# Five-stage transformer kernel on one Trainium2 core: two elementwise products and the low halves of the dispatch weights move from VectorE to GpSimd, and the input comes in three transfers

## The reference, cut to what matters

```python
x = x + 0.5 * L0_ffn(layernorm(x))     # fp4 feed-forward, "f0"
x = x + L0_attn(layernorm(x))          # decayed linear attention, "a0"
x = x + 0.5 * L0_ffn(layernorm(x))     # "f0" again
x = x + 0.5 * L1_ffn(layernorm(x))     # soft mixture of experts, "f1"
x = x + L1_attn(layernorm(x))          # causal softmax attention, 16 heads, "a1"
x = x + 0.5 * L1_ffn(layernorm(x))     # "f1" again

def fp4_quant_dequant(x):              # blocks of 16 along the last dimension
    scale = max(max(abs(xb)) / 6, 1e-12)
    idx = searchsorted(MID, abs(xb / scale))
    return GRID[idx] * sign(xb) * scale

def L0_ffn(x):                         # every operand is quantized first
    h = silu(q(x) @ q(w_gate).T) * (q(x) @ q(w_up).T)      # 704 wide
    return q(h) @ q(w_down).T

def L1_ffn(x):                         # 8 experts of 128 slots = 1024 slots
    logits = rms_norm(x, gamma_x) @ rms_norm(slot_embeds, gamma_slot).T
    dispatch = softmax of logits over the 8 experts
    slots = dispatch.T @ xn
    out = softmax over all 1024 slots of logits @ (gelu(slots @ w1) @ w2)
```

## Time and profile before

| What | Value |
|---|---|
| median of 3 executions | 2931.3 us |
| the profiled execution's own time | 2929.66 us |
| its span in the profile | 2927.6 us |
| PE / PEld busy | 2429.8 / 1846.8 us (83% / 63%) |
| DVE busy | 2108.1 us (72%) |
| ACT busy | 1625.4 us (56%) |
| POOL busy | 1096.1 us (37%) |
| mean granted clock of PE | 0.935 of 2.4 GHz |

### The profile page before, as it was taken

The page is one execution under the profiler, slowest core; times in us unless marked ns, Lnnn a source line. Parts: engine busy times, 40 slices in busy tenths (PEclk is TensorE's granted clock), DMA queues, the critical chain, the costliest instruction groups (busy, mean ns, idle before and its releaser), DMA issues.

```text
span 2927.6 us, 56018 instructions
## 1 busy us (share of the span) xinstructions
PE 2429.8 (83%) x23228; PEld 1846.8 (63%) x23228; DVE 2108.1 (72%) x3530; ACT 1625.4 (56%) x2761; POOL 1096.1 (37%) x791
## 2 busy tenths in 40 slices
PE   1677777778888988889889889889898888898888
PEld 0445555555666766657567666667666667677666
DVE  6599999889898886777877777776786765343432
ACT  2244544454765757365566556574656566556554
POOL 0144544444352443244443526262525252222112
PEclk9799998899999999989898999999989999999999
DMA  4000000000000000000000000000000000000000
GB/s 153 17 1 1 1 1 1 1 1 1 1 1 1 1 1 1 23 13 12 11 14 2 23 2 23 2 23 2 23 9 21 12 2 8 8 8 1 8 8 8
DMA packets 34572, 32.96 MB, mean 11 GB/s; under 512 B 7377, under 2 KB 33681, under 8 KB 34321
## 3 DMA queue, kind: packets, MB, share of 16 engines
q1 hardware_dynamic: 34320, 29.40, 3.1%
HBM read 12.34 MB, written 4.19 MB: 6 GB/s over the span
## 4 chain that ended last, share of the span: by engine, by line
PE 44%; DVE 17%; ACT 6%; issue 4%; POOL 4%; SPq 1%; DMA 1%; POOLq 0%; DVEq 0%; ACTq 0%
PE psum L623 11%; PE psum L625 10%; PE psum L624 10%; PE psum L629 3%; PE psum L1055 2%; DVE a1pr L1771 2%; PE psum L1057 2%; PE psum L1056 2%; POOL f1hT L2042 2%; PE psum L906 1%; PE psum L959 1%; DVE f1d L1882 1%; DVE a1c L1789 1%; PE psum L936 1%; DVE f1e L1886 1%
## 5 line engine op out<-in xcount | busy, mean ns | idle before, releaser
L2042 POOL TENSOR_TENSOR f1hT<-f1g,f1hT 128x512 f16<-128x512 f32 x256 | 311.7, 1224 | 677.1 <-ACT f1hT L1422 676.6
L2029 POOL TENSOR_TENSOR a1pr<-a1PT,a1pr 128x1024 f16<-128x1024 f32 (+1 forms) x176 | 350.3, 1992 | 334.9 <-DVE a1pr L1771 334.9
L623 PE MATMUL psum<-f1sl,f1w1h 128*128 128x256 f16 x1024 | 290.4, 284 | 30.7 <-DVE f1pr L1929 16.6
L623 PE MATMUL psum<-f1w2h,f1hT 128*128 128x256 f16 x1024 | 282.4, 276 | 17.0 <-POOL f1hT L2042 15.2
L624 PE MATMUL psum<-f1sl,f1w1h 128*128 128x256 f16 x1024 | 290.0, 283 | 0.0
L625 PE MATMUL psum<-f1sl,f1w1l 128*128 128x256 f16 x1024 | 289.7, 283 | 0.0
L624 PE MATMUL psum<-f1w2l,f1hT 128*128 128x256 f16 x1024 | 281.6, 275 | 0.0
L625 PE MATMUL psum<-f1w2h,f1hT 128*128 128x256 f16 x1024 | 281.4, 275 | 0.0
L1748 DVE TENSOR_REDUCE a1nm<-psum 128x2 f32<-128x768 f32 (+3 forms) x176 | 198.1, 1125 | 79.1 <-PE psum L886 77.7
L2006 POOL TENSOR_TENSOR f0hT<-f0Y,f0hT 128x512 f16<-128x512 f32 (+1 forms) x128 | 139.6, 1105 | 181.4 <-ACT f0Y L1214 181.4
L1771 DVE CAST a1pr<-a1PT 128x1024 f16<-128x1024 f32 (+1 forms) x176 | 156.0, 891 | 69.5 <-ACT a1PT L1318 49.5
(11 more groups left out here) (335 smaller groups left out, 7502.1 us busy)
## 6 DMA issues: line engine op xcount, KB each, us to landing
a1Q<-a1st SPq DMA_DIRECT2D x96, 64.0 KB, 2.6
a1K<-a1st SPq DMA_DIRECT2D x96, 64.0 KB, 2.5
x<-in_L_attn_x SPq DMA_DIRECT2D x8, 512.0 KB, 8.8
out<-x SPq DMA_DIRECT2D x8, 512.0 KB, 3.0
wslot<-in_L_ffn_w SPq DMA_DIRECT2D x1, 1024.0 KB, 7.5
wraw<-in_L_ffn_w SPq DMA_DIRECT2D x1, 1024.0 KB, 5.7
wslot<-in_L_ffn_slot_embeds SPq DMA_DIRECT2D x1, 1024.0 KB, 8.2
a1Q<-a1mr SPq DMA_DIRECT2D x64, 4.0 KB, 1.7
```

The source lines that it names most:

```text
L623: e.matmul(out, lh, rh, start=start, stop=False)
L2029: e.tensor_tensor(a1["pr"][:, i % 2, 1, :, 0:w], a1["PT"][:, i % 2, :, 0:w], a1["pr"][:, i % 2, 0, :, 0:w], ALU.subtract).then_inc(s["a1_pl"])
L2042: e.tensor_tensor(hT1[:, 1, 2 * hp:2 * hp + 2, :], gg[:, hp % 2, :, :], hT1[:, 0, 2 * hp:2 * hp + 2, :], ALU.subtract).then_inc(s["f1_hl"])
```

## The change

- `f0_tokens`, `f0_hidden`: the first product Y goes to POOL (`f0_products`, the new `f0_scaled`). What was one instruction with a scalar and a tensor factor becomes a small one of DVE, r = r * (-TIE), and a product of POOL. Two semaphores, `f0_xp` and `f0_hp`, tell DVE that Y is there; `f0_xm` and `f0_hm` now count two for each tile, one for r and one for M.
- `f1_weights`: the low half goes from DVE to POOL, with the same signal `f1_el`.
- `load`: sequence 0 alone, then sequences 1 to 3 in one transfer, then 4 to 7 in one; the last two are due behind the other weights. They are a chain of their own.

```diff
--- before.py
+++ after.py
@@ -396,10 +396,10 @@
         for name in (
                 "dve", "w_dma", "w_dma2", "w_dma3", "w_qm", "w_qr", "w_q", "w_sq", "w_pw", "w_se", "w_T", "w_h", "w_l", "w_b",
                 "w_sh", "w_sl", "w_k",
-                "xin0", "xin1", "xin2", "xin3", "out",
+                "xin0", "xin1", "xin2", "out",
                 "ln_ve", "ln_rs", "a0_ve", "a0_rs",
-                "f0_xm", "f0_xr", "f0_xy", "f0_xq", "f0_xT", "f0_xh", "f0_xl", "f0_g", "f0_u", "f0_si", "f0_th",
-                "f0_hm", "f0_hr", "f0_hy", "f0_hq", "f0_hT", "f0_hY", "f0_hl", "f0_dn", "f0_xu",
+                "f0_xp", "f0_xm", "f0_xr", "f0_xy", "f0_xq", "f0_xT", "f0_xh", "f0_xl", "f0_g", "f0_u", "f0_si", "f0_th",
+                "f0_hp", "f0_hm", "f0_hr", "f0_hy", "f0_hq", "f0_hT", "f0_hY", "f0_hl", "f0_dn", "f0_xu",
                 "a0_xn", "a0_xT", "a0_xh", "a0_xl", "a0_pj", "a0_sg", "a0_qr", "a0_qh", "a0_ql", "a0_kh", "a0_kl",
                 "a0_v", "a0_kt", "a0_a", "a0_vf", "a0_vb", "a0_vh", "a0_vl", "a0_nh", "a0_nl", "a0_af", "a0_ah",
                 "a0_al", "a0_y", "a0_yh", "a0_yl", "a0_kv", "a0_S", "a0_Sh", "a0_Sl", "a0_o", "a0_xu",
@@ -538,10 +538,9 @@
         def sync(e, q, banks):
 
             def load(b):
-                yield 0.5 if b < 2 else 6.0 + b
-                if b >= 4:
-                    q.wait_ge(f"xin{b % 4}", 16)
-                e.dma_start(xb[:, b, :, :], x_d[:, b, :, :]).then_inc(s[f"xin{b % 4}"], 16)
+                yield (0.5, 6.0, 9.0)[b]
+                bs = (slice(0, 1), slice(1, 4), slice(4, 8))[b]
+                e.dma_start(xb[:, bs, :, :], x_d[:, bs, :, :]).then_inc(s[f"xin{b}"], 16)
 
             def store(b):
                 yield at_f1(B + b) + 152.0
@@ -610,7 +609,7 @@
                 yield 1.0e6
                 q.wait_ge("out", 16 * B)
 
-            return [weights(), *[chain(z, B) for z in (load, a1_moves, store)], last()]
+            return [weights(), chain(load, 3), *[chain(z, B) for z in (a1_moves, store)], last()]
 
 
 
@@ -1173,7 +1172,7 @@
                     n = 2 * f + tp
                     yield S + 4.0 + 20.0 * tp
                     q.wait_ge("w_dma", 96)
-                    q.wait_ge("f0_xm", n + 1)
+                    q.wait_ge("f0_xm", 2 * n + 2)
                     e.activation(f0["Mx"][:, :], f0["Mx"][:, :], ACT.Relu, scale=MAGIC, bias=cst[:, C_MAG:C_MAG + 1]).then_inc(s["f0_xr"])
                     yield S + 7.8 + 20.0 * tp
                     q.wait_ge("f0_xT", n + 1)
@@ -1194,7 +1193,7 @@
                     e.activation(f0["h"][:, ft % 3, :].rearrange("p (i n) -> p i n", i=2), psum[:, 0:2, 0:FH], ACT.Silu,
                                  scale=1.0 / (XS * WS)).then_inc(s["f0_si"])
                     yield G + 8.0
-                    q.wait_ge("f0_hm", ft + 1)
+                    q.wait_ge("f0_hm", 2 * ft + 2)
                     m2 = f0["M"][:, t % 2, :]
                     e.activation(m2, m2, ACT.Relu, scale=MAGIC, bias=cst[:, C_MAG:C_MAG + 1]).then_inc(s["f0_hr"])
 
@@ -1541,7 +1540,7 @@
                 b = f % B
                 yield S
                 if f < B:
-                    q.wait_ge(f"xin{b % 4}", 16 * (b // 4 + 1))
+                    q.wait_ge(f"xin{(b > 0) + (b > 3)}", 16)
                 else:
                     q.wait_ge("a0_xu", 4 * b + 4)
                 normalize("x", b, "ln_ve")
@@ -1564,10 +1563,11 @@
                     q.wait_ge("dve", q.tick())
                     e.reciprocal(r_, c_).then_inc(s["dve"])
                     q.wait_ge("dve", q.tick())
-                    e.scalar_tensor_tensor(blocks16(Yx), blocks16(v), -TIE, bc(r_, 16), ALU.mult, ALU.mult).then_inc(s["dve"])
-                    q.wait_ge("dve", q.tick())
+                    e.tensor_scalar(r_, r_, -TIE, None, ALU.mult).then_inc(s["f0_xm"])
+                    yield S + 4.4 + 20.0 * tp
+                    q.wait_ge("f0_xp", n + 1)
                     e.tensor_scalar(Mx.bitcast(u32), Yx.bitcast(u32), 0x7F800000, None, ALU.bitwise_and).then_inc(s["f0_xm"])
-                    yield S + 4.6 + 20.0 * tp
+                    yield S + 5.6 + 20.0 * tp
                     q.wait_ge("f0_xr", n + 1)
                     e.scalar_tensor_tensor(Yx, Mx, MAGIC, Yx, ALU.add, ALU.add).then_inc(s["dve"])
                     q.wait_ge("dve", q.tick())
@@ -1602,10 +1602,9 @@
                     q.wait_ge("dve", q.tick())
                     e.reciprocal(r_, c_).then_inc(s["dve"])
                     q.wait_ge("dve", q.tick())
-                    e.scalar_tensor_tensor(blocks16(Y), blocks16(h), -TIE, bc(r_, 16), ALU.mult, ALU.mult).then_inc(s["dve"])
-                    k = q.tick()
-                    yield G + 7.2
-                    q.wait_ge("dve", k)
+                    e.tensor_scalar(r_, r_, -TIE, None, ALU.mult).then_inc(s["f0_hm"])
+                    yield G + 8.0
+                    q.wait_ge("f0_hp", ft + 1)
                     e.tensor_scalar(M.bitcast(u32), Y.bitcast(u32), 0x7F800000, None, ALU.bitwise_and).then_inc(s["f0_hm"])
                     yield G + 9.2
                     q.wait_ge("f0_hr", ft + 1)
@@ -1881,9 +1880,6 @@
                     q.wait_ge("f1_el", n)
                     e.tensor_tensor(d3, Lg[:, :, jp * 256:(jp + 1) * 256], psum[:, 4, 0:2 * P].unsqueeze(1).broadcast_to([P, NT, 2 * P]),
                                     ALU.subtract).then_inc(s["f1_ds"])
-                    yield E + 4.0
-                    q.wait_ge("f1_eh", n + 1)
-                    e.tensor_tensor(e1[:, jp % 2, 1, :, :], d3, e1[:, jp % 2, 0, :, :], ALU.subtract).then_inc(s["f1_el"])
 
             def f1_slots(j):
                 S = at_f1(j)
@@ -1980,9 +1976,21 @@
                 S = at_f0(f)
                 v = f0["xh"][:, :, :].rearrange("p t d -> p (t d)")
                 for tp in range(2):
+                    yield S + 3.2 + 20.0 * tp
+                    q.wait_ge("f0_xm", 2 * (2 * f + tp) + 1)
+                    e.tensor_tensor(blocks16(f0["Yx"][:, :]), blocks16(v), bc(f0["scx"][:, 1, :], 16), ALU.mult).then_inc(s["f0_xp"])
                     yield S + 5.6 + 20.0 * tp
                     q.wait_ge("f0_xy", 2 * f + tp + 1)
                     e.tensor_tensor(blocks16(v), blocks16(f0["Yx"][:, :]), bc(f0["scx"][:, 0, :], 16), ALU.mult).then_inc(s["f0_xq"])
+
+            def f0_scaled(f):
+                S = at_f0(f)
+                for t in range(NT):
+                    ft = 4 * f + t
+                    yield S + 10.0 + 10.0 * t + 6.4
+                    q.wait_ge("f0_hm", 2 * ft + 1)
+                    e.tensor_tensor(blocks16(f0["Y"][:, t % 2, 0:F]), blocks16(f0["h"][:, ft % 3, :]), bc(f0["sc"][:, t % 2, 1, :], 16),
+                                    ALU.mult).then_inc(s["f0_hp"])
 
             def f0_hidden(f):
                 S = at_f0(f)
@@ -2029,6 +2037,15 @@
                         e.tensor_tensor(a1["pr"][:, i % 2, 1, :, 0:w], a1["PT"][:, i % 2, :, 0:w], a1["pr"][:, i % 2, 0, :, 0:w],
                                         ALU.subtract).then_inc(s["a1_pl"])
 
+            def f1_weights(j):
+                S = at_f1(j)
+                d3 = dd[:, :].rearrange("p (t n) -> p t n", t=NT)
+                for jp in range(4):
+                    n = 4 * j + jp
+                    yield S + 36.0 + 8.0 * jp + 4.0
+                    q.wait_ge("f1_eh", n + 1)
+                    e.tensor_tensor(e1[:, jp % 2, 1, :, :], d3, e1[:, jp % 2, 0, :, :], ALU.subtract).then_inc(s["f1_el"])
+
             def f1_powers(j):
                 yield at_f1(j) + 2.0
                 powers("p", "f1_ve", "f1_rs", j + 1, True)
@@ -2042,9 +2059,9 @@
                         e.tensor_tensor(hT1[:, 1, 2 * hp:2 * hp + 2, :], gg[:, hp % 2, :, :], hT1[:, 0, 2 * hp:2 * hp + 2, :],
                                         ALU.subtract).then_inc(s["f1_hl"])
 
-            return [weights(), *[chain(z, 2 * B) for z in (f0_powers, f0_products, f0_hidden, f0_halves)],
+            return [weights(), *[chain(z, 2 * B) for z in (f0_powers, f0_products, f0_scaled, f0_hidden, f0_halves)],
                   *[chain(z, B) for z in (a0_powers, a0_values, a1_powers, a1_probs)],
-                  *[chain(z, 2 * B) for z in (f1_powers, f1_mlp)]]
+                  *[chain(z, 2 * B) for z in (f1_powers, f1_weights, f1_mlp)]]
 
         order, _ = rehearse({"sp": sync, "pool": gpsimd, "act": scalar, "dve": vector, "pe": tensor}, s)
         block = ctx.enter_context(nc.Block())
```

## The result

The changed kernel took 2966.8 us (median of four executions, 2963.9 to 2969.0) against 2931.8: ratio 1.0119, 95% interval 1.0101 to 1.0136. It is 35 us slower; 2916 was forecast, with 2886 to 2952 as the range.

The account below looks back on a forecast made before the run. DVE was taken to bound A, DVE and PE 700 to 1150 us, PE's waits D. -17 - 10 + 3 + 9.5 - 1 = -15.5 us from 2931.3 gave 2916 us, range 2886 to 2952.

Parts of the forecast that it names:

- Steps 1 to 4: First products and low halves leave DVE for POOL; each us of POOL's work costs DVE 0.22 us.
- R2: Rival: contention with POOL takes the gain up to 1150 us, from 0.53 us of DVE per POOL us; 2943 us, chance 0.14.
- Step 5: A: 22.3 us less of DVE's time, 5 us lost to 57 new waits on POOL: -17 us.
- step 6: 700 to 1150 us: 24.5 us less of DVE, but PE soon takes over as bound: -10 us.
- A: Window 100 to 700 us, f0 beside a0; DVE, busy 89%, was said to carry it; -17 us.
- Step 7: C: the low half comes 1.05 us later, but PE has other matmuls meanwhile: +3 us, bounds 0 and 34.
- C: Window 1150 to 2400 us, a1 beside f1; PE busy 88%, DVE 74%; +3 us.
- Step 8: D: the low half stands in front of PE's start; 9 waits, each 1.05 us longer: +9.5 us.
- D: Window from 2400 us, f1 alone; PE busy 86%, the chain PE waits for is bare; +9.5 us.
- Step 9: Start of the run: input in three transfers, so the weights ACT waits for come sooner: -1 us.
- R3: Rival: low half on POOL lengthens f1 throughout C and D; +27 us, 2958 us, chance 0.11.
- R4: Rival: nothing measurable, DVE's relief in A partly becomes waits on POOL; +2 to -5, 2929 us, chance 0.20.

Follow-up runs that it names:

- e7: Instructions of the kernel before, but with the input in three transfers, performed in the order planned for the changed kernel; 2974.1 us, ratio 1.0150.
- e16: e7 repeated in the order of e12: instructions of the kernel before, order planned for the changed kernel; 2934.4 us, ratio 1.0011.
- e12: The changed kernel, instructions unchanged, planned with 125 ns in place of 120 for the lag of DVE's signals; 2933.5 us, ratio 1.0008.
- e8: The kernel before with only the 704-wide first product on POOL, all queues keeping the order planned for the kernel before; 2978.6 us, ratio 1.0160.
- e5: The kernel before with only the low halves on POOL, all queues keeping the order planned for the kernel before; 2942.7 us, ratio 1.0041.
- e1: The kernel before with the input in three transfers and nothing else; 2929.9 us, ratio 0.9993.
- e4: The kernel before, no instruction changed, planned with 130 ns in place of 110 for POOL's lag; 2917.3 us, ratio 0.9950.

## Why the prediction was wrong, point by point

- **Steps 1 to 4: the parts held, their sum only by luck.** DVE's busy time fell by 47.0 us up to 1150 us; 22.3 + 24.5 = 46.8 were worked out. But a part of the 47.0 comes with the new order and with work that slid behind 1150 us: with the order held it is 26.5 us (e7) and 27.5 us (e16 and e12). The products take 1.44 and 1.20 us on POOL in the mean, the low half 2.16 (1.39, 1.06 and 2.15 were taken; the first two are medians). The mask's mean rose from 715 to 866 ns: the collision with POOL is real. With the order held and over the whole run, DVE lost 73 us by it for 245 us of new work on POOL in e7's order, and 68 for 244 in that of e12: 0.30 and 0.28 us for one (worked out from the instructions that went and came and DVE's busy times), where 0.22 was taken. That is under R2's 0.53, and R2 did not decide.
- **Step 5 failed, and step 6 with it.** The step went from "DVE is busy 89% of A" to "DVE's work is nearly the length of A" and took 17 us for 22. The relief came as idle time of DVE: busy 23.2 us less in A, with the stage no shorter and f0's last mask 20 us later. With the order held, the two moves together gave 7 to 9 us (e7) and 1 us or none (e16), where the sum, without the transfers, had 14.5. Its last sentence, 5 us for 57 waits since ready work stands behind them, was wrong too: in e8, 48 of 64 waits are exposed for 62.8 us, because the order is fixed and the work that is ready does not stand at the head of the queue. In the changed kernel the planner put the masks later and only 10 of 63 waited (10.8 us), and the time went to the other waits of the chain.
- **The sentence that the orders "can shift waits by some 10 us either way" was the mis-sized term.** It is +44 us in e7, 33 us between the changed kernel and e12, and 38 us between plans of the kernel before. It stood outside the sum and the range; it should have been the first term of the range.
- **Step 7.** PE's waits at the dispatch matmuls in C are 5.5 and 4.0 us in the changed kernel, by L1881 and L1907, and 0.9 us by POOL's low half: 10.4 us for 1.9, over the 10 that step 7 had named as its sign of being wrong. In e5 the stage cost about 6 us (its f1 passes start 1 us late at 1139 us and 7 us late at 2365), but PE's waits at these matmuls are 2.1 us there: the +3 was near in size, and where e5 pays is not shown.

```profile
PE psum L1054 <- DVE f1d L1881: 5.5, 9, 0.9
...
PE psum L1054 <- DVE f1eT L1907: 4.0, 4, 2.0
...
PE psum L1054 <- POOL f1e L2047: 0.9, 1, 0.9
```

- **Step 8 held where its order held.** Two waits a pass, 1.05 us each, gives 8.4 us for eight; e5 has 29.1 - 23.6 = 5.5 us: the first wait of a pass grew by 0.96 us, the second, 1.98 to 2.53, by 0.55. With step 7's 3 I had 12.5 for C and D, and e5 as a whole has +12, an agreement that is partly luck, since the waits of step 7 did not show in e5 and those of step 8 were 5.5. In the changed kernel the +9.5 did not come: from the pass that starts at 2472 us before, and at 2508 here, to the end it is 456 us in both. "D keeps its length because the order has changed there" had been named as a sign of being wrong. The new order has other matmuls there, and PE's eight waits, 23.6 us, became four, 19.2 us:

```profile
PE psum L1054 <- DVE f1d L1881: 19.2, 4, 5.4
PE psum L622 <- DVE f1pr L1925: 11.0, 9, 1.5
```

- **Step 9.** ACT starts at 19.38 us in place of 20.63 us; -1 was taken, e1 has -2 with an interval that holds 0.
- **R3** had the sign and 2958 us, but not by its mechanism: PE's idle time at the first dispatch matmul over the whole run grew from 37.9 to 44.5 us, not by 55, and e7 loses more with no low half on POOL at all. Its nearness is chance. With the order held, R4 came nearest: the relief showed as idle time of DVE, but only 10.8 us of it as the mask's waits on POOL.

What stays open: which pieces of the new order cost the time. The f1 pass that starts at 1278 us before starts 30 us later in the changed kernel and 34 in e7; the gap shrinks to 8 and 15 us at the pass of 1754 and grows again to 37 and 46 by the pass of 2472. In e12 the last mask is 17.5 us late as well, but the pass of 1754 starts 12 us early, so the end of f0 does not decide. No run isolates a piece of the order. Nor was a kernel tried whose planner knows that DVE stands still beside POOL.

## What to carry to other kernels

Before work is moved off the busiest engine, ask whether that engine has idle time at the head of its queue, and whether the move puts a new wait there: if it waits for a hand-over, its busy share is no measure of what a relief brings, and a move that adds a hand-over to the chain can cost more than it frees. When a program's order comes out of a planner, time several plans of both versions that differ in a number without meaning, and then perform one version's instructions in the other's order; the spread between plans is the noise against which the change is judged. That spread is also worth harvesting by itself.

## What the runs showed of the hardware that was not expected

PE's busy time is not a constant of the program: the same 23228 matmuls took 2425.3 us in the profiled execution of e4 and 2455.3 us in that of e7. A part goes with the mean granted clock (0.940 and 0.932), which differs between executions of one program as well: the 79 of the kernel before have 0.928 to 0.944. But the changed kernel was busy 12.9 us longer than the kernel before at the higher clock of the two (0.937 for 0.935). Lost overlap where a run of matmuls is broken would fit that; no run isolates it.

In the collisions of DVE and POOL, DVE bears the larger part. The mean less the median, times the count, added up over all groups by shape from 100 to 1150 us of the changed kernel, is 98 us for DVE and 43 for POOL (101 and 40 before, 78 and 40 in e7). The moved work puts 136 us more on POOL there than in e7, and POOL's sum is 3 us higher. The price for DVE, 0.28 to 0.30 us for one of POOL with the order held, can itself be moved by an order: in e7 DVE is busy 31 us less than before for the same instructions.
